# Routed experts: rest columns' products ahead of the first columns', one group of transposes, down products of both halves behind it, third chunk padded to 128 rows

## What is computed

```python
g = jnp.einsum('ecd,eid->eci', buf, W1).astype(jnp.float32)
u = jnp.einsum('ecd,eid->eci', buf, W3).astype(jnp.float32)
h = (jax.nn.silu(g) * u).astype(xt.dtype)
out = jnp.einsum('eci,edi->ecd', h, W2)
y_pairs = out[e, posc] * (w.reshape(-1) * valid)[:, None]
```

## Time and profile before

| | |
|---|---|
| median of 3 runs | 496.58 us (496.21 to 497.57) |
| profiled execution, its own time | 497.83 us |
| its span in the trace | 496.0 us |
| granted TensorE clock, mean | 0.981 |
| TensorE busy | 464.3 us, 94% |
| VectorE / ScalarE / GpSimd busy | 67% / 52% / 42% |
| steps 0 to 15 of stage 3 | 273.4 to about 488.5 us |

### The profile page before, as it was taken

One profiled execution on the slowest core, in us unless ns is written; L12 is line 12 of the kernel. 1 busy time (PEld: TensorE's weight loads), 2 busy tenths in 40 slices (PEclk: granted clock), 3 DMA queues, 4 the chain that ended last, 5 costly groups with the idle time before them and its releaser, 6 DMA issues.

```text
span 496.0 us, 7772 instructions
## 1 busy us (share of the span) xinstructions
PE 464.3 (94%) x2496; PEld 393.5 (79%) x2496; DVE 329.9 (67%) x707; ACT 257.8 (52%) x379; POOL 208.2 (42%) x175
## 2 busy tenths in 40 slices
PE   1889999999999939999999999999999999999993
PEld 1358887888888728888888999999999999888982
DVE  5669998998987534358937976666666666666520
ACT  4744544545553333363253576666666666666531
POOL 0612443664334733541636724444427444332242
PEclk9989999999999969999999999999999999999997
DMA  8626545666545713233629999998969988897545
GB/s 320 233 82 234 170 152 168 233 233 223 169 174 199 246 56 113 86 50 48 85 65 230 211 301 313 234 258 255 261 225 264 280 268 247 259 258 223 107 58 70
DMA packets 29164, 95.02 MB, mean 192 GB/s; under 512 B 4816, under 2 KB 5328, under 8 KB 28624
## 3 DMA queue, kind: packets, MB, share of 16 engines
q0 software_dynamic: 17040, 43.66, 35.4%
q1 hardware_dynamic: 11808, 50.98, 30.8%
q10 hardware_dynamic: 288, 0.01, 0.0%
HBM read 67.50 MB, written 28.70 MB: 194 GB/s over the span
## 4 chain that ended last, share of the span: by engine, by line
PE 84%; DVE 7%; issue 3%; DMA 2%; ACT 1%; another core or an unknown queue 1%; POOLq 0%; POOL 0%; DVEq 0%; ACTq 0%
PE psG L1251 46%; PE psY L1251 28%; PE psT L1256 6%; PE psG L1495 1%; DMA front<-in_x,idx 1%; ACT arena L619 1%; DMA tok_i<-in_ids 1%; DVE stats L908 1%; DVE xh_sb L881 1%; DVE gu L897 1%; DVE arena L886 0%; PE psG L1279 0%; DVE stats L915 0%; DVE big L834 0%
## 5 line engine op out<-in xcount | busy, mean ns | idle before, releaser
L1251 PE MATMUL psY<-arena 128*128 (+2 forms) x372 | 94.4, 401 | 0.0
L1251 PEld LDWEIGHTS psY<-arena 128*128 128x128 f32 (+1 forms) x372 | 67.5, 188 | 13.3
L497 POOL DMA_INDIRECT ht<-out,idx x32 | 34.6, 1081 | 78.2 <-PE psT L1256 62.4
L1251 PE MATMUL psY<-slot,arena 128*128 128x512 f32 (+1 forms) x240 | 61.1, 399 | 0.0
L1026 DVE TENSOR_TENSOR slot<-raw,slot 128x1536 fp32r<-128x1536 f32 x25 | 43.9, 1757 | 23.8 <-ACT slot L615 23.1
L1251 PE MATMUL psG<-arena 128*128 x228 | 58.0, 403 | 0.0
L1026 DVE TENSOR_TENSOR arena<-raw,arena 128x1536 fp32r<-128x1536 f32 x24 | 42.1, 1758 | 22.9 <-ACT arena L615 19.5
L1251 PE MATMUL psG<-arena,slot 128*128 128x512 f32 x216 | 52.6, 399 | 0.0
L1251 PEld LDWEIGHTS psY<-slot,arena 128*128 128x128 f32 (+1 forms) x240 | 43.7, 189 | 9.0 <-ACT xh_sb L659 0.3
L1251 PEld LDWEIGHTS psG<-arena 128*128 128x128 f32 x228 | 42.0, 190 | 10.2 <-issue 1.9
L1251 PEld LDWEIGHTS psG<-arena,slot 128*128 128x128 f32 x216 | 41.1, 193 | 8.5
(11 more groups left out here) (221 smaller groups left out, 809.1 us busy)
## 6 DMA issues: line engine op xcount, KB each, us to landing
raw<-in_w SPq DMA_DIRECT2D x51, 768.0 KB
padded<-xh_sb SPq DMA_DIRECT2D x19, 256.0 KB
raw<-in_ctx_t SPq DMA_DIRECT2D x2, 1024.0 KB, 8.9
ht<-in_ctx_t SPq DMA_DIRECT2D x1, 1024.0 KB, 13.3
xh_sb<-in_ctx_t SPq DMA_DIRECT2D x1, 1024.0 KB, 15.4
out<-log_sb SPq DMA_DIRECT2D x4, 256.0 KB
ht<-out,idx POOLq DMA_INDIRECT x32
xb<-in_x,idx POOLq DMA_INDIRECT x19
```

The source lines that it names most:

```text
L497: pool.indirect_dma_start(ht[:, n, :], None, halves_of_out, slots(e * NA + a, 0)).then_inc(g_here[n], 16)
L1251: ins = pe.matmul(ps, left[a], right[b], start=n == 0 and m == 0, stop=n == total - 1 and m == 2)
```

## The change

TensorE now does `rest_up(e, 0)`, `rest_up(e, 1)`, `first_up(e)`, `gathered(e + 1)`, `rest_transposed(e)` and then both down products. All steps have this order, the last one without the gather and with `first_up` at the end as before. ScalarE's and VectorE's lists follow. The rest's hidden values are stored at a pitch of 256 columns (`H0 + a * CAP`), of which 224 are written in each step and 32 are set to zero once by a memset ahead of stage 3, so that all four transposes are 128 wide and all down products contract over 128 rows. The weights' rows behind row 96 of the third chunk are zeros of the host's layout, before as now.

```diff
@@ TensorE: out3
-                    o, w = c * CAP + a * P, P if c < 2 else WIDTH[1]
-                    left = [hid[0:w, 1 - r, m, o:o + P] for m in range(2)]
-                    right = [piece(s, 2)[0:w, c * D:(c + 1) * D] for s in SLOT[r]]
+                    o = c * CAP + a * P
+                    left = [hid[:, 1 - r, m, o:o + P] for m in range(2)]
+                    right = [piece(s, 2)[:, c * D:(c + 1) * D] for s in SLOT[r]]
@@ TensorE: rest_transposed
-                pe.wait_ge(hid3, e * NI + rest_at(known, 1) + 1)
+                pe.wait_ge(hid3, e * NI + NA)
...
-                        ins = pe.transpose(psG[3][0:WIDTH[c], o:o + P],
-                                           rest_of(gu, a)[:, c * P:c * P + WIDTH[c]], ident)
+                        s = H0 + a * CAP + c * P
+                        ins = pe.transpose(psG[3][:, o:o + P], gu[:, s:s + P], ident)
@@ TensorE: step
-                if known != E2 - 1:
-                    first_up(e, r, known)
                 rest_up(e, r, 0, known)
                 rest_up(e, r, 1, known)
                 if known != E2 - 1:
+                    first_up(e, r, known)
                     gathered(e + 1, 1 - r, False)
+                rest_transposed(e, known)
...
                     down3(e - 1, r, 0, last)
-                rest_transposed(e, known)
-                if known != 0:
                     down3(e - 1, r, 1, last)
@@ ScalarE: step
                 if more:
                     split(e + 2, 1, r)
-                    silu(first, s_sb[:, 0:CAP], psG[0][:, 0:CAP])
+                silu(0, rest_of(s_sb, 0), psG[1][:, 0:REST])
                 if known != 0:
                     act.wait_ge(y3_ps, e * NA - NA)
                 split(e + 1, 2, 1 - r)
+                silu(1, rest_of(s_sb, 1), psG[2][:, 0:REST])
+                if more:
+                    silu_first()
+                    gathered(e + 1)
+                high_rest()
+                if known == 0:
+                    rows(NJ - 1)
                 if more:
                     high_first()
...
                 if known is None or known + 3 <= E2:
                     split(e + 3, 0, 1 - r)
                 if known != 0:
-                    rows3(e - 1, 1 - r, 0, last)
-                high_rest()
-                if known != 0:
-                    rows3(e - 1, 1 - r, 1, last)
+                    for a in range(NA):
+                        rows3(e - 1, 1 - r, a, last)
@@ VectorE: ahead of stage 3
             hidden(11)
+            dve.wait_ge(hid_lo, len(SEQ))
+            dve.memset(gu[:, H0:H0 + NA * CAP].rearrange("p (a n) -> p a n", a=NA)[:, :, REST:CAP], 0.0)
             gathered(0)
@@ VectorE: step
                 if more:
                     split(e + 2, 1, r)
+                gate_rest(0)
+                split(e + 1, 2, 1 - r)
+                gate_rest(1)
+                if more:
                     gate_first()
-                    split(e + 1, 2, 1 - r)
-                    low_first()
-                    gate_rest(0)
-                    gate_rest(1)
                     gathered(e + 1)
...
+                low_rest()
...
+                if more:
+                    low_first()
                 if known is None or known + 3 <= E2:
                     split(e + 3, 0, 1 - r)
-                low_rest()
```

More of the change, by code:

```diff
@@ L135, in gated_layer @@
         REST = I_MLP - P
-        WIDTH = [P, REST - P]
         H0 = CAP
@@ L342, in rest_of @@
         def rest_of(ap, a):
[L343 to L351, removed]
+            return ap[:, H0 + a * CAP:H0 + a * CAP + REST]
+        FIRST3 = 2
         @block.sync
@@ L723, in step @@
                 more = known is None or known + 1 < E2
-                first, rest = first_at(known), [rest_at(known, a) for a in range(NA)]
                 last = None if known is None else known - 1
@@ L731, in silu, with silu_first @@
                     act.activation(dst, src, ACT.Silu).then_inc(silu3, 1)
+                def silu_first():
+                    silu(FIRST3, s_sb[:, 0:CAP], psG[0][:, 0:CAP])
                 def high_first():
-                    act.wait_ge(hid3, e * NI + first + 1)
+                    act.wait_ge(hid3, e * NI + FIRST3 + 1)
                     act.activation(hid[:, r, 0, 0:CAP], gu[:, 0:CAP], ACT.Copy).then_inc(hid3_hi, 1)
@@ L1191, in step @@
                 more = known is None or known + 1 < E2
-                first, rest = first_at(known), [rest_at(known, a) for a in range(NA)]
                 def gate_first():
-                    dve.wait_ge(silu3, e * NI + first + 1)
+                    dve.wait_ge(silu3, e * NI + FIRST3 + 1)
                     if known != 0:
-                        dve.wait_ge(hid3_lo, e * 2 - 1)
+                        dve.wait_ge(hid3_lo, e * 2)
                     dve.tensor_tensor(gu[:, 0:CAP], s_sb[:, 0:CAP], psG[0][:, CAP:2 * CAP], ALU.mult).then_inc(hid3, 1)
                 def gate_rest(a):
-                    dve.wait_ge(silu3, e * NI + rest[a] + 1)
+                    dve.wait_ge(silu3, e * NI + a + 1)
                     if known != 0 and a == 0:
@@ L1207, in low_first @@
                 def low_first():
-                    dve.wait_ge(hid3_hi, e * 2 + 1 + (not more))
+                    dve.wait_ge(hid3_hi, e * 2 + 2)
                     dve.tensor_tensor(hid[:, r, 1, 0:CAP], gu[:, 0:CAP], as_f32(hid[:, r, 0, 0:CAP]),
@@ L1212, in low_rest @@
                 def low_rest():
-                    dve.wait_ge(hid3_hi, e * 2 + 1 + more)
+                    dve.wait_ge(hid3_hi, e * 2 + 1)
                     dve.tensor_tensor(hid[:, r, 1, CAP:NI * CAP], psG[3][:, :], as_f32(hid[:, r, 0, CAP:NI * CAP]),
@@ L1470, in first_up @@
                 if known != 0:
-                    pe.wait_ge(hid3, (e - 1) * NI + 1)
+                    pe.wait_ge(hid3, e * NI)
                 for m in range(2):
@@ L1479, in rest_up @@
                 if known != 0:
-                    pe.wait_ge(hid3, (e - 1) * NI + a + 2)
+                    pe.wait_ge(hid3, (e - 1) * NI + a + 1)
                 ps = psG[1 + a][:, 0:2 * REST].rearrange("p (c i) -> p c i", c=2)
```

## The result

The changed kernel takes 497.17 us (median of 22 runs, 496.32 to 498.20), the one before 496.26 us (22 runs, 495.38 to 497.57). The ratio is 1.0016, with a 95% interval of 1.0009 to 1.0022: slower by 0.8 us, where 0.9 us was forecast, and within the 0.3% that was called no change.

A forecast was written before the change was run, and what follows sets the result against it. TensorE, busy for 94% of the span, was taken to bound the kernel. Terms -1.05 + 0 + 0.3 + 1.65 = +0.9 us on the median of 496.58 gave 497.5 us, range 496.0 to 499.0.

The forecast's parts named there:

- Order and count of products: Stage 3, TensorE: the same products are issued and turning the up products round changes neither length; 0.
- Padding: Stage 3 down products: 128 rows instead of 96 cost nothing and may give back up to 0.05 us for nine.
- One run of 18: Routed steps: one transpose group, then 18 unbroken down products, gains 0.07 us a step for 15 steps, -1.05 us.
- Steps 1 to 14 without a wait: Loop steps: the second gate has 2 us to spare before the transposes, so TensorE does not wait; 0.
- Step 0: First step of stage 3: TensorE waits for the second gate, delayed by the memset; +0.3 us, bounds 0.05 and 0.6.
- Last step: Last step: TensorE idles before the transposes for silu, weight piece and second gate; +1.65 us, bounds 1.0 and 1.8.
- The three slower rivals: Stage 3: uneven runs, late weights, or a clock fall after the last step's idle time; chance 0.27 together.
- the runs did even out: Rival said stage 3 runs do not even out, so the gain is 0 and time 498.5 us; chance 0.17.
- no weights came late: Rival said piece 0's later load delays one to two steps by 0.8 us each, 498.5 to 499 us; chance 0.06.
- a granted clock of 1.00: Rival said TensorE drops to 1.2 GHz after the last step's idle time, 2.5 us more, 500.0 us; chance 0.04.
- The faster rival: Stage 3: without 96-row chunks the up products speed up too, 0.34 us a step in all, 493.1 us; chance 0.07.

The follow-up runs named there:

- all_between: The changed kernel with the rest's transposes between the two groups of nine down products in all steps from 1 on; 0.9987 of the kernel before.
- pad_only: The kernel before with the padding alone (pitch of 256, memset, 128-wide transposes, 128-row products), all orders as before; 0.9993 of the kernel before.
- double_low: last_between with one more VectorE pass over a weight piece ahead of its low part in steps 1 to 14; 483.87 us against 483.38, ratio 1.0013.
- triple_low: last_between with two more VectorE passes over a weight piece ahead of its low part in steps 1 to 14; 503.78 us against 483.38, ratio 1.0426.
- gates_ahead: The changed kernel with VectorE's last-step weight piece moved behind both gates of the rest; 495.77 us against 495.73 for the kernel before, ratio 0.9991.
- last_between: The changed kernel with the last step's four transposes back between its two groups of nine down products; 494.88 us against 495.73, ratio 0.9982.

## Why the prediction was right

The forecast was 497.5 us, 0.9 above the median; measured is a difference of 0.8 us. By its own steps:

- **Order and count of products, 0.** Nearly so: the order of the up products gives 0.005 us a step (`all_between` against `pad_only`).
- **Padding, 0, or up to 0.05 us for nine products.** This term was put at the wrong end of its bounds: alone it gives 0.47 us in 14 steps, 0.017 us for nine. The rule of the Trainium skill (TensorEngine Tiling (Array Packing), Key Properties) that a change of tiling mode drains the engine was weighed rightly: a drain for each 96-row chunk is not there, since leaving the 96 rows in the changed kernel costs 0.023 us a step with four changes of rows in it.
- **One run of 18, -1.05 us.** The number was met, its making was not. Steps 1 to 14 give -1.06 us, but 0.52 of it is grouping, and the rest is padding and the order of the up products: grouping by itself was put at twice what it gives. The sum came right because it was taken from runs of stage 2 that had both, 18 products in 4.18 to 4.21 us; measured 4.22. There is luck in it too. The forecast counts 15 steps of 0.07 us; 14 steps gave 0.076 each and the last one gave nothing, since its first nine down products stood behind up products before the change and took only 2.09 us (476.63 to 478.72). Down products and transposes together take 4.63 us there in both kernels, the wait left out (476.63 to 481.26, 476.90 to 481.53). The estimate from the 216 ns of the Trainium skill (TensorE: Matmul & The Clock Gate, Back-to-back issue gap) does not add up as written: 18 products in 3.9 us would give 15 x 0.38 = 5.7 us, not about 5. The 4.22 us speak against it either way.
- **Steps 1 to 14 without a wait.** No wait is listed. In the loop the second gate ends 2.1 us before it is wanted, as `double_low` and `triple_low` confirm. Later weight loads cost TensorE nothing.
- **Step 0, +0.3 us.** Too large, and mostly not a wait: the step is 0.11 us longer. The memset takes 0.11 us and not 0.19, and its delay is gone before the routed step begins: VectorE starts its two weight pieces 2.88 us after TensorE's stage 3 in both traces (276.31 - 273.43 and 275.89 - 273.01). The second gate is then done at 281.56, just ahead of the transposes at 281.63. By comparison with other rows, some 0.08 us of the 0.11 are the transposes' new place, ahead of the routing products: eight transposes take 0.79 us ahead of a down product (304.96 to 305.75 in `pad_only`), 0.87 ahead of other transposes (293.39 to 294.26) and 0.88 ahead of the routing products (281.19 to 282.07 in the kernel before).

```profile
266.37 0.11 DVE L1160 MEMSET gu<- 128x64 f32 x1
...
275.89 3.41 DVE L1021 TENSOR_TENSOR slot<-raw,slot 128x1536 fp32r<-128x1536 f32 x2
...
281.19 0.37 DVE L1201 TENSOR_TENSOR gu<-s_sb,psG 128x224 f32<-128x224 f32 x1
```

- **Last step, +1.65 us.** Measured 1.63, by the path that was described. `gates_ahead` gives the lower bound, 1.0 us forecast and 1.02 measured, and `last_between` shows that nothing behind it gives the time back or takes it over.

The three slower rivals did not come: the runs did even out, no weights came late, and after 1.6 us of idle time 18 down products still took 4.22 us (477.31 to 481.53), with a granted clock of 1.00 from 475.27 to 484.40, the 2.4 GHz level. The faster rival, up products that speed up as well, falls too: 24 of 448 columns take 4.88 us and 24 of 256 columns 2.87 us, as before.

## What to carry to other kernels

A reordering that is good in a loop's middle steps has to be costed in its first and last step by itself, because the work that covers a wait is missing there; here one step of 16 cost more than the 14 good ones gave. With the last step's order left as it was (`last_between`) the same change is 1.0 us shorter than the kernel before in the trace of stage 3, and its time is 0.9982 of it (0.9965 to 0.9999). On an engine that never waits, what a reordering can still gain are the small differences in pace between runs of instructions, and they can be read from long runs elsewhere in the same trace. And the room ahead of a wait can be measured: add work to the waiting side until the busy engine stops.

## What the runs showed of the hardware

- A run of 512-column products is uneven at first and then goes at 227 ns from start to start. Nine in a run's later part take 2.04 us (267.31 to 269.35), the first nine behind up products 2.08 us (474.77 to 476.85 in `last_between`), the first nine behind transposes 2.14 to 2.19 us. Part of the last figure is a shift of 0.08 us at the seam: the transposes ahead of the products are that much shorter, 0.79 us for eight where they take 0.87 ahead of more transposes. With 96-row products in it a run of 18 takes 4.23 to 4.25 us, where it takes 4.22. Why it begins unevenly was not settled.
- Contracting over 128 rows instead of 96 costs TensorE nothing; it even gives 0.02 us for nine products.
- The level of the whole kernel differed by 12 us between sets of runs (495.7 and 483.4 us for the kernel before). The traces of `double_low` and `triple_low` lack a break near 173 us that all the others have: TensorE idle for 5.8 to 10.1 us, 7.87 in the kernel before, and then a granted clock of 0.50, the 1.2 GHz level (181 to 186 us). Step 1 starts at 271.67 in `double_low` and at 285.63 in the changed kernel. The break lies ahead of stage 3 and in the kernel before as well; its length can add to the spread of the times, and the terms that were read within stage 3 hold none of it. What makes it was not settled.
